# Bfloat16 copies of the attention contexts on GpSimd in place of ScalarE, in a four-layer kernel with hand-ordered engines

## What is computed

```python
gate_v = _get_sel_gate(x, sel_v_w, rs)
gate_o = _get_sel_gate(x, sel_o_w, rs)
xv = jnp.einsum('bsd,hedp->bshep', x, v_w.reshape(H, E, D, P))
v = jnp.einsum('bshep,bshe->bhsp', xv, gate_v)
att = jax.nn.softmax(jnp.einsum('bhqp,bhkp->bhqk', q, k) * SCALE, axis=-1)
ctx = jnp.einsum('bhqk,bhkp->bqhp', att, v)
weighted = ctx[:, :, :, None, :] * gate_o[..., None]
out = jnp.einsum('bshep,hepd->bsd', weighted, o_w.reshape(H, E, P, D))
```

## Time and profile before

| What | Value |
|---|---|
| runs | 1480.16, 1480.84, 1483.44 us |
| profiled execution | 1481.03 us; its span 1479.2 us |
| TensorE matmul (PE) busy | 1404.5 us, 95% of the span |
| VectorE (DVE) busy | 1283.9 us, 87% |
| ScalarE (ACT) busy | 1275.8 us, 86% |
| GpSimd (POOL) busy | 859.0 us, 58% |
| chain that ended last | PE 62%, ACT 13%, DVE 11%, POOL 7%, issue 4%, SyncE's queue 2% |

### The profile page before, as it was taken

One profiled execution on the slowest core, in us unless ns is written; L12 is line 12 of the kernel. 1 busy time (PEld: TensorE's weight loads), 2 busy tenths in 40 slices (PEclk: granted clock), 3 DMA queues, 4 the chain that ended last, 5 costly groups with the idle time before them and its releaser, 6 DMA issues.

```text
span 1479.2 us, 34876 instructions
## 1 busy us (share of the span) xinstructions
PE 1404.5 (95%) x9748; PEld 963.9 (65%) x9905; DVE 1283.9 (87%) x5266; ACT 1275.8 (86%) x4428; POOL 859.0 (58%) x1345
## 2 busy tenths in 40 slices
PE   4678999999999999999999999999999999999998
PEld 2455666666676666667666666766666676666654
DVE  3677988998998999899899999989999998998886
ACT  3657888899988889998888999888899988889886
POOL 3113656556565656656565565656556565655567
PEclk8689999999999999999999999999999999999999
DMA  4410000000000000000000000000000000000000
GB/s 136 139 56 16 10 14 16 15 15 12 15 11 14 16 15 15 12 15 11 14 16 15 15 13 15 11 14 16 15 15 13 15 11 14 14 15 7 8 3 4
DMA packets 68960, 30.18 MB, mean 20 GB/s; under 512 B 19168, under 2 KB 68768, under 8 KB 68768
## 3 DMA queue, kind: packets, MB, share of 16 engines
q1 hardware_dynamic: 51552, 19.31, 4.9%
q10 hardware_dynamic: 17216, 8.65, 2.1%
HBM read 17.31 MB, written 2.10 MB: 13 GB/s over the span
## 4 chain that ended last, share of the span: by engine, by line
PE 62%; ACT 13%; DVE 11%; POOL 7%; issue 4%; SPq 2%; DMA 1%; POOLq 0%; ACTq 0%; another core or an unknown queue 0%; DVEq 0%
PE psC L309 43%; PE psA L309 7%; PE psB L309 6%; DVE nmA L2240 5%; ACT PTA L1344 3%; ACT PS L1344 3%; POOL accO L3405 3%; DVE PTB L2365 3%; ACT TE L1344 3%; DVE TE L2497 2%; ACT PTB L1344 2%; SPq L3776 2%; PE psA L421 1%; POOL accO L3413 1%; PE psB L553 1%
## 5 line engine op out<-in xcount | busy, mean ns | idle before, releaser
L3405 POOL TENSOR_TENSOR accO<-accO,TE 128x512 f32<-128x512 f32 x192 | 246.3, 1283 | 143.9 <-DVE TE L2497 137.7
L1344 ACT ACTIVATE TE<-psC,gate 128x128 f32<-128x128 f32 x1024 | 300.1, 406 | 17.7 <-PE psC L309 10.4
L1344 ACT ACTIVATE TE<-psC,gateO 128x128 f32<-128x128 f32 x1024 | 292.5, 375 | 24.8 <-PE psC L309 16.2
L2497 DVE SCALAR_TENSOR_TENSOR TE<-psC,gate,TE 128x128 f32<-128x128 f32 x1024 | 284.5, 339 | 29.5 <-PE psC L309 18.4
L2497 DVE SCALAR_TENSOR_TENSOR TE<-psC,gateO,TE 128x128 f32<-128x128 f32 x1024 | 287.1, 341 | 13.2 <-PE psC L309 8.2
L3393 POOL TENSOR_TENSOR TE<-TE 128x256 f32<-128x256 f32 x256 | 192.4, 752 | 164.5 <-DVE TE L2497 160.4
L309 PE MATMUL psC<-Vh,xTh 128*128 128x512 f32 x512 | 263.3, 514 | 2.3 <-ACT PS L1344 1.2
L309 PE MATMUL psC<-Oh,ch 128*128 128x512 f32 x512 | 262.9, 513 | 0.2
L309 PE MATMUL psC<-Oh,cl 128*128 128x512 f32 x512 | 203.0, 396 | 0.0
L309 PE MATMUL psC<-Vh,xTl 128*128 128x512 f32 x512 | 202.5, 396 | 0.0
L309 PE MATMUL psC<-Ol,cb 128*128 128x512 bf16 x452 | 176.2, 390 | 0.0
(11 more groups left out here) (228 smaller groups left out, 3426.7 us busy)
## 6 DMA issues: line engine op xcount, KB each, us to landing
bdB<-Kc SPq DMA_DIRECT2D x384, 16.0 KB
raw<-in_L_ffn_v_w ACTq DMA_DIRECT2D x8, 512.0 KB, 4.5
raw<-in_L_ffn_o_w ACTq DMA_DIRECT2D x8, 512.0 KB, 4.2
x_sb<-in_x SPq DMA_DIRECT2D x32, 64.0 KB, 2.1
ctx_sb<-in_ctx SPq DMA_DIRECT2D x32, 64.0 KB, 2.0
bdA<-Kc SPq DMA_DIRECT2D x128, 8.0 KB
Qb<-Qc SPq DMA_DIRECT2D x128, 8.0 KB
bias_sb<-in_mask_Bx1xSxS_ff SPq DMA_DIRECT2D x32, 64.0 KB, 1.9
```

What stands on the lines that cost most here:

```text
L1344: return A.activation(o, i, func, **kw)
L2497: m = V.scalar_tensor_tensor(TE[:, i, e], psC[:, p, e * P:(e + 1) * P], gates[:, e:e + 1], TE[:, i, e], ALU.mult, ALU.add)
L3405: G.tensor_tensor(accO[:], TE[:, slot(b, H1)] if h == 1 else accO[:], TE[:, slot(b, H1 + h)], ALU.add).then_inc(o_fe, 1)
```

## The change

GpSimd makes `cb` in the place of ScalarE, with a semaphore of its own, `c_cb`. The statistics of the second layer norm get tiles of their own (`stA2`, `mvA2`, `rsA2`; before, they were shared with the first). The sequences of all five engines are new.

```diff
+        stA2 = sb("stA2", [P, 6])
+        mvA2 = sb("mvA2", [P, 2])
+        rsA2 = sb("rsA2", [P, 1])
...
-                    pe.wait_ge(c_ch, 4 * b + 2 * (h // 4) + 2)
+                    pe.wait_ge(c_ch, 2 * b + h // 4 + 1)
+                    pe.wait_ge(c_cb, 2 * b + h // 4 + 1)
                     pe.wait_ge(c_cl, 2 * b + h // 4 + 1)
...
-            def c_short(b, i):
-                if b not in BATCHES:
-                    return
-                act.wait_ge(c_ch, 4 * b + 2 * i + 1)
-                copy(four(cb_, i), f(four(ch, i))).then_inc(c_ch, 1)
...
-                spread(x1[:], stA, mvA, rsA, a_ln2, b, n)
+                spread(x1[:], stA2, mvA2, rsA2, a_ln2, b, n)
...
-                dve.wait_ge(c_ch, 4 * b + 2 * i + 1)
+                dve.wait_ge(c_ch, 2 * b + i + 1)
...
+            def c_short(b, i):
+                if b not in BATCHES:
+                    return
+                pool.wait_ge(c_ch, 2 * b + i + 1)
+                pool.wait_ge(o_ps, 2 * H1 * (b - 1) + 8 * i + 8)
+                G.tensor_copy(four(cb_, i), f(four(ch, i))).then_inc(c_cb, 1)
```

In GpSimd's period `c_short` stands between the additions of the values:

```diff
                 values(i - 6, 4, 0)
+                c_short(i - 6, 0)
+                a_root2(i - 3)
                 values(i - 6, 4, 1)
...
                 values(i - 6, 7, 1)
+                c_short(i - 6, 1)
```

More of the change, by code:

```diff
@@ L708, in start @@
                 a_shared(0)
+                b_values(0)
                 a_ht(0)
@@ L939, in start @@
                 a_ht(4)
-                b_values(4)
                 outputs(1, 2, 1)
                 a_ffn(4)
+                a_ctxt(5)
                 outputs(1, 2, 0)
-                a_ctxt(5)
                 outputs(1, 3, 1)
@@ L1675, in start @@
                 cut(8)
+                a_values2(1)
                 b_queries(0)
-                a_values2(1)
+                b_values(0)
                 cut(9)
                 b_exp(0, 0)
+                b_exp(0, 1)
                 cut(10)
-                b_exp(0, 1)
                 b_trans(0, 0)
@@ L1704, in start @@
                 a_shared(1, 1)
-                b_values(1)
                 a_ht(1)
@@ L1794, in start @@
                 c_context(0, 1)
+                outputs(0, 1)
                 a_shared(3, 0)
                 a_shared(3, 1)
-                outputs(0, 1)
                 a_ht(3)
+                a_ctxt(4)
                 outputs(0, 2)
-                a_ctxt(4)
+                b_values(3)
                 a_keys(4)
                 a_xt(4)
-                c_short(0, 1)
                 outputs(0, 3)
@@ L2029, in period @@
-                c_context(i - 3, 0)
-                values(i - 3, 6)
-                c_short(i - 3, 0)
-                values(i - 3, 7)
-                a_x1t(i)
-                outputs(i - 3, 0)
-            def end():
+            def end():
+                a_exp(B - 1, 0)
+                a_exp(B - 1, 1)
+                b_trans(B - 2, 3)
+                a_values2(B - 1)
+                a_exp(B - 1, 2)
+                a_exp(B - 1, 3)
+                values(B - 4, 1)
+                c_exp(B - 3, 0)
+                a_unnorm(B - 1)
+                b_unnorm(B - 2)
+                c_exp(B - 3, 1)
+                values(B - 4, 2)
+                values(B - 4, 3)
+                a_att(B - 1)
+                values(B - 4, 4)
+                b_att(B - 2)
+                a_proj(B - 1)
+                values(B - 4, 5)
+                c_context(B - 4, 0)
+                values(B - 4, 6)
+                values(B - 4, 7)
+                a_x1t(B - 1)
+                outputs(B - 4, 0)
+                b_keys(B - 1)
@@ L2560, in start @@
                 a_routed(0, 2)
+                b_keys(0)
+                a_stats(1, 2)
+                a_norm(1)
                 cut(5)
@@ L3088, in end @@
-                a_stats2(B - 1, 2)
-                c_stats(B - 2, 0)
+                a_first(B - 1, 1)
+                a_stats2(B - 1, 0)
+                values(B - 4, 5)
+                c_context(B - 4, 0)
+                c_share(B - 3, 2)
+                a_stats2(B - 1, 1)
+                a_stats2(B - 1, 2)
+                b_third(B - 2)
                 values(B - 4, 6)
                 a_norm2(B - 1)
+                c_share(B - 3, 3)
+                c_stats(B - 2, 0)
                 values(B - 4, 7)
```

1302 lines of the change are left out of this document (636 added, 666 removed).

## The result

The changed kernel takes 1497.42 us, the median of four runs from 1496.14 to 1498.07. The ratio to the kernel before is 1.0105, with a 95% interval from 1.0088 to 1.0123: 15 to 16 us slower than the kernel before, whose median of four runs beside it is 1481.5 us, where I had forecast no difference. The range ended at 1488.0, so the measured time lies above it.

The account below looks back on a forecast made before the run. A 43.12 us period was taken as ScalarE's 18.75, 0.14 between, and TensorE's 24.23. 1481.03 - 2.6 (periods) + 0 + 2.0 (start) + 0.3 (end) = 1480.7, predicted as 1480.5 us since the runs' median is 0.2 lower; range 1471 to 1488.

Parts of the forecast that it names:

- The copies leave ScalarE: Sixty-four copies, 40.9 us busy, leave ScalarE where it waits for TensorE anyway; gain 0.
- The copy takes 0.65 us on GpSimd: Length of one moved copy on GpSimd, estimated from similar operations: 0.65 us, between 0.52 and 1.28.
- The second `c_context` is not held up: GpSimd finishes head 7 before TensorE's second `c_context` needs it, 0.5 us to spare; steady-state cost 0.
- the waits that I subtracted: GpSimd's 1.09 us of waits for VectorE, taken off 5.96 us to leave 4.87 of work behind the copy.
- So 18.75 us stay: ScalarE's unbroken stretch of the period holds the same 26 steps in another order, so its 18.75 us stay.
- So 24.23 us stay, but for small waits: TensorE's stretch, `values(b, 3, 1)` to `outputs(b, 6, 1)`, holds the same steps, so its 24.23 us stay.
- my 0.1: Small TensorE waits, such as for `a_ctxt`, shrink: 0.1 us off each of 26 periods, -2.6 us.
- the wait in front of the scores: VectorE's 0.76 us wait for the first layer's first score tile; its chain starts some 0.6 us sooner, gain 0.
- Rival 4: Each GpSimd copy waits for one VectorE instruction, exceeding the cover by 0.2 us a period: 1485.7 us; chance 0.04.
- The 0.69 us: Length of a VectorE instruction of `Q`'s or `nmA`'s kind, assumed as each GpSimd copy's wait under port exclusion.
- The start: Before the steady state: first scores 3.6 us later, partly offset by earlier loads; +2.0 us, between -2 and +4.5.
- The end: Last batches: GpSimd's copy falls mostly into its wait for VectorE; +0.3 us, between 0 and 1.3.

Follow-up runs that it names:

- k_best2: Kernel before, own second-layer-norm tiles, GpSimd's copy behind the layer-norm roots, TensorE waiting for `cb` only at the matmul reading it: 1483.42 us, ratio 1.0000.
- k_act: Changed kernel with its new order, but ScalarE makes the copies `cb` again: 1496.88 us, ratio 1.0096.
- k_pv: Changed kernel with one piece of TensorE's period as before (last layer's scores, `values(i - 4, 1, 0)`, `b_pvs`, `a_pvs`): 1529.48 us, ratio 1.0317.
- b_split: Kernel before with one TensorE move, `c_scores(i - 3, 1)` put between `b_pvs` and `a_pvs`: 1498.13 us, ratio 1.0105.
- k_fix: Changed kernel, TensorE's `a_pvs` one expert half earlier and VectorE's `c_choice(i - 3, 8)` behind `a_attend` and `b_attend`: 1496.04 us, ratio 1.0090.

## Why the prediction was wrong

- **The copies leave ScalarE, gain 0.** Right: `k_best2` has them on GpSimd, a ratio of 1.0000 and a period of 43.17.
- **The copy takes 0.65 us on GpSimd.** It took 0.608. The second `c_context` is not held up, as said. The place was looked at for TensorE's second `c_context` alone. I had counted the copy from `ch` and left out that GpSimd, early at that place, waits for `ch` with the copy, 0.99 us in the trace of the change; the waits that I subtracted were the room in which it could be early. In the old order that wait costs 1.0 us in a period through `a_root2`; in the new order `a_root2` stands directly behind the copy and the cost is nil (`k_act` against the change: 43.45 both).
- **"So 18.75 us stay."** This step failed, by 0.18 (18.89 with the 0.14 between the engines, 19.07 now). I compared which steps stand in ScalarE's stretch and not what they wait for. Counted from the first values half behind `PTC`, `a_pvs` starts 9.64 us later before (734.78 to 744.42) and 9.87 now (875.18 to 885.05), and ScalarE waits for it with `UA`. `k_pv` and `b_split` give the price: 1.12 us of such waits cost 1.25 in the period, 0.53 cost 0.64. By the trace VectorE's `atb`, late behind `gt`, ends together with this path.
- **"So 24.23 us stay, but for small waits."** This failed by 0.15, and the sign of my 0.1 was wrong. 0.11 of it are transposes that come to `PTA` as VectorE finishes it. I had called the wait in front of the scores, taken away by the new order, the kind of thing to look for, and did not look for the waits that it adds.
- **Rival 4, the exclusion of VectorE, had 0.04.** I tied it to the copy on GpSimd. It acts where the new order puts GpSimd's additions beside VectorE's two-input operations, with or without that copy. The 0.69 us were also taken from `Q` and `nmA`, which read PSUM and take 0.69 beside a GpSimd operation or without one.
- **The start:** +2.0 us forecast. The first scores begin at 24.94 against 20.92, 4.0 us later for the 3.6 of the sum; the first contexts are 2.8 later, and 2.6 more are lost by batch 3. The sign was right and the size less than half; the sum had nothing for what is lost between batch 0 and batch 3. **The end:** +0.3 forecast, 1.8 seen.
- The sum by the steps as they were measured: 25 x 0.33 + 5.4 + 1.8 + 1.0 of longer single periods = 16.5 us, against 16.6 between the spans.

What stays open: of the 0.33 us, 0.18 and 0.15 are placed and `k_fix` won back 0.08. In `k_fix` 0.14 of the 0.18 are gone, while TensorE's stretch is 0.06 longer, and no run took out the 0.25 that are left there (0.04 and 0.21). No run here was faster than the kernel before.

## What to carry to other kernels

When the order of a tuned pipeline changes, list for each engine in the stretch that sets the period what every step waits for, in both orders; the same set of steps in another order is not the same stretch. A cheap operation moved to an idle engine costs what queues behind its wait: put it where its input has long come, and let the consumer wait only at the instruction that reads it. If taking out one wait gains nothing, read the trace again: another may stand just behind it, and only both together show.

## What the runs showed of the hardware

VectorE's operations with two inputs in SBUF did not run beside GpSimd's additions, which read SBUF too. In the changed kernel `gsum<-best` (128x16) took 0.47 us at 854.37, until GpSimd's operation from 854.20 to 854.80 was over, where it takes 0.16 when it is not held, and `gp<-first,gp` took 0.71 at 884.53 beside GpSimd's addition from 884.31 to 885.09, 0.27 in the kernel before (at 745.40):

```profile
854.37 0.47 DVE L2424 TENSOR_TENSOR gsum<-best 128x16 f32<-128x16 f32 x1
...
884.53 0.71 DVE L2403 SCALAR_TENSOR_TENSOR gp<-first,gp 128x128 f32<-128x128 f32 x1
...
854.20 0.60 POOL L3388 TENSOR_TENSOR v_sb<-TE 128x128 f32<-128x128 f32 x1
...
884.31 0.78 POOL L3383 TENSOR_TENSOR TE<-TE 128x256 f32<-128x256 f32 x1
```

`gt` and `gap` above behave alike. The Trainium skill (SBUF — State Buffer, "SBUF: two separate sides") says that the pair of ports is locked for a whole instruction and the other engine blocks fully; the trace agrees, for these additions, and it shows the blocked time as busy time of the blocked instruction, not as idle time. Of some 120 two-input operations of VectorE in the changed kernel that start inside an addition `TE<-TE` or `v_sb<-TE`, 0.25 us or more before its end, one ended before it. GpSimd's roots (128x1) and its `keyrow` (16x128) did not hold them where they met: `best<-best,gsum` took 0.18 at 250.11, inside a root from 249.85 to 250.40. It goes the other way too. In the kernel before, `gsum<-best` starts 0.04 us behind GpSimd's addition of 711.36 and takes its 0.16, and that addition takes 0.80; all 26 additions beside this `gsum` take 0.80, the others mostly 0.73 or 0.74.

This is a part of why VectorE's busy time rose by 46.0 us with no work added. The durations of its instructions add up to 24.7 us more (1486.2 to 1510.9). The forms that grew are mainly `gp`, `gsum`, `gt`, `first`, `xnC` and `gap`; others that were held in the kernel before are held less, `best<-best,gsum` (332 ns before, 192 now) and `gateO` (432 and 211). The rest of the 46.0 is that the records overlap less. It is also why the idle times of the kernel before, where I had looked for such a port, could not show it: in the prediction I wrote that GpSimd has no idle time to blame on it, while these two forms and `gap` (344 ns) showed the holding already. The price is to be read from the mean duration of two-input forms.

A second thing: TensorE, busy for 18.64 of 19.01 us (98%), was not the bound in ScalarE's stretch. 0.23 us less work in it changed neither kernel.
